# Turned rows for two FFN runs, smaller rings of drives and decays, and the gate's values in the hidden buffer, in a hybrid attention, FFN and state-space kernel

## The reference, cut to what matters

```python
x = x + attention(layernorm(x), ...)     # gated delta rule, 32 heads
x = x + ffn(layernorm(x), ...)           # layer 0 of the FFN
x = x + state_space(layernorm(x), ...)   # 16 states for each of 512 channels
x = x + ffn(layernorm(x), ...)           # layer 1, the same weights

def ffn(x):                              # weights unpacked from 4 bits, INNER = 1408
    gate, up = x @ w_gate.T, x @ w_up.T
    y = (silu(gate) * up) @ w_down.T
    return y / sqrt(mean(y * y, -1) + 1e-6)

def state_space(x):
    dt = softplus(x @ dt_w + dt_b); B, C = split(x @ bc_w.T + bc_b)
    h = exp(dt * A) * h + (dt * x) * B   # step by step along the sequence
    return (h * C).sum(states) @ out_w.T + out_b
```

## Time and profile before

| what | us |
|---|---|
| median of three runs | 4284.56 |
| the profiled execution | 4285.06 |
| its span | 4283.4 |
| joint stage with scans (3249 to 4113): length, PE busy, DVE busy | 864.0, 831.2, 786.5 |
| after the last scan (4113 to the end): length, PE busy, DVE busy | 170.4, 159.2, 23.1 |

### The profile page before, as it was taken

How to read it: one execution, slowest core, us unless ns; L and a number is a source line. 1 busy time by engine, 2 the same in 40 slices (tenths; PEclk the granted TensorE clock), 3 DMA queues, 4 the chain that set the end, 5 groups by cost and what they waited for, 6 DMA issues and landing times. The chain is left out here.

```text
span 4283.4 us, 82747 instructions
## 1 busy us (share of the span) xinstructions
PE 4131.2 (96%) x30773; PEld 2542.0 (59%) x30773; DVE 3402.7 (79%) x8648; ACT 2295.7 (54%) x5351; POOL 460.5 (11%) x470
## 2 busy tenths in 40 slices
PE   7899999999999999999999999998899999999999
PEld 4566666666666666666666666666444444444444
DVE  4888888888888888888888888886547989888950
ACT  3555555555555555555555555554445655554543
POOL 0111111111111111111111111111000000000000
PEclk9999999999999999999999999999999999999999
DMA  2111111111111012111011011010104445444520
GB/s 75 42 34 35 38 37 37 34 38 33 36 43 33 31 41 75 58 43 33 31 38 38 31 43 33 31 39 10 66 1 129 160 139 175 150 149 146 174 69 10
DMA packets 202467, 263.50 MB, mean 62 GB/s; under 512 B 18222, under 2 KB 101426, under 8 KB 202066
## 3 DMA queue, kind: packets, MB, share of 16 engines
q1 hardware_dynamic: 202066, 258.20, 18.9%
HBM read 249.24 MB, written 8.91 MB: 60 GB/s over the span
## 5 line engine op out<-in xcount | busy, mean ns | idle before, releaser
L516 PE MATMUL bank<-x_blocks,w_qkv 128*128 128x512 f32 x2048 | 927.3, 596 | 4.9 <-ACT raw L810 4.2
L516 PEld LDWEIGHTS bank<-x_blocks,w_qkv 128*128 128x128 f32 x2048 | 375.7, 192 | 394.5 <-issue 375.6
L1126 DVE SCALAR_TENSOR_TENSOR conv<-raw,conv_w,conv 128x1024 f32<-128x1024 f32 x384 | 516.1, 1344 | 71.2 <-ACT conv L784 62.1
L642 PE MATMUL bank<-w_out_unit,oT 128*128 128x512 f32 x1008 | 492.3, 611 | 15.2 <-ACT oT L858 15.2
L598 PE MATMUL bank<-w_z_unit,x_blocks 128*128 128x256 f32 x2048 | 488.5, 382 | 0.0
L598 PEld LDWEIGHTS bank<-w_z_unit,x_blocks 128*128 128x128 f32 x2048 | 372.0, 192 | 40.8 <-issue 0.2
L1371 PE MATMUL bank<-xnT_f,w_gu 128*128 128x512 f32 x704 | 330.3, 613 | 9.1 <-ACT xnT_f L1861 8.2
L810 ACT COPY raw<-bank 128x512 f32<-128x512 f32 x256 | 149.0, 582 | 323.7 <-PE bank L516 321.0
L1389 PE MATMUL bank<-w_down,hidden 128*128 128x512 f32 x704 | 319.5, 597 | 2.8 <-DVE hidden L1411 2.8
L1379 PE MATMUL bank<-xnT_f,w_gu 128*128 128x512 f32 x704 | 316.8, 593 | 0.6 <-DVE hidden L1411 0.5
L907 ACT ACTIVATE k_scaled<-o 128x128 f32<-128x128 f32 x512 | 153.9, 302 | 301.6 <-DVE o L1176 261.5
(11 more groups left out here) (245 smaller groups left out, 7785.1 us busy)
## 6 DMA issues: line engine op xcount, KB each, us to landing
rows_b<-bc_rows SPq DMA_DIRECT2D x256, 256.0 KB, 3.4
rows_c<-bc_rows SPq DMA_DIRECT2D x256, 256.0 KB, 3.5
w_qkv<-in_w_qkv SPq DMA_DIRECT2D x128, 256.0 KB, 2.9
decay<-gc_rows SPq DMA_DIRECT2D x64, 512.0 KB, 3.9
w_z_unit<-in_w_z SPq DMA_DIRECT2D x32, 512.0 KB, 4.4
w_out_unit<-in_w_out SPq DMA_DIRECT2D x32, 512.0 KB, 5.0
x_after<-x SPq DMA_DIRECT2D x16, 256.0 KB, 2.0
x_blocks<-x_after SPq DMA_DIRECT2D x4, 1024.0 KB, 10.1
```

Source lines behind the costliest of these rows:

```text
L516: made = e.matmul(PROJ[:, :], w_qkv[:, p % 2, j, :], xnT[:, n // HK, j, h * BANK:(h + 1) * BANK], start=j == 0, stop=j == KT - 1)
L642: made = e.matmul(out_rows(N, t)[:, :], turned_to(N, t)[:, r, :], w_out[:, N % 2, r, :], start=r == 0, stop=r == REP - 1)
L1126: e.scalar_tensor_tensor(acc, raw[:, i % 2, tap:tap + T], conv_w[:, tap, col:col + 1], acc, ALU.mult, ALU.add).then_inc(on["conv"], 1)
```

## The change

Seven things change, all in `second_half`:

1. `xnT_f` gets two buffers, by run parity, and `gate` is gone: silu writes into `hidden`, and the hidden product is made in place. silu no longer waits for the hidden product of the tile before, but for the down product of two tiles before. `drive` has 6 buffers in place of 8, `step_decay` 3 in place of 4.
2. The decay of step p + 2 therefore waits for the scan of step p - 1, in place of p - 2, and a drive for the sum of the pair six steps back, in place of eight.
3. `SUM_LAG` is 3 in place of 4: sums of pairs and the turns and copies of `y` come one slot earlier.
4. The four turns of a run stand in four slots (start - 5 to start - 2), all through WB, in place of two slots with two each (start - 4 and start - 3) through WB and the gate's bank.
5. Statistics come one slot earlier relative to the run's start, one tile per slot for runs 2 to 6.
6. `RUN_START` moves: run 2 from 43 to 46, run 3 from 91 to 92, run 4 stays at 136, run 5 from 183 to 184, run 6 from 230 to 235, run 7 from 279 to 281. The scans keep their slots (8 to 263).
7. In run 0's part the rows of run 1 are normalized and turned a little earlier, and run 0's last down product comes last.

```diff
-RUN_START = {1: 0, 2: 43, 3: 91, 4: 136, 5: 183, 6: 230, 7: 279}
-SUM_LAG, DRIVE_RING, H_RING = 4, 8, 3
+RUN_START = {1: 0, 2: 46, 3: 92, 4: 136, 5: 184, 6: 235, 7: 281}
+SUM_LAG, DRIVE_RING, H_RING, DECAY_RING = 3, 6, 3, 3
-        uses += [(at - 4 + t // 2, 1, ("ffn_turn", R, t)) for t in range(TILES)]
+        uses += [(at - 5 + t, 1, ("ffn_turn", R, t)) for t in range(TILES)]
-        xnT, xn = sb("xnT_f", [P, KT, BANK]), sb("xn_f", [P, 2, D])
+        xnT, xn = sb("xnT_f", [P, 2, KT, BANK]), sb("xn_f", [P, 2, D])
-        gate, hidden = sb("gate", [P, BANK]), sb("hidden", [P, 2, BANK])
+        hidden = sb("hidden", [P, 2, BANK])
...
 (silu_gate)
-            if U > 0:
-                e.wait_ge(on["hidden"], U)
-            e.activation(gate[:, :], GB[:, :], ACT.Silu).then_inc(on["gate_silu"], 1)
+            if U >= 2:
+                e.wait_ge(on["down_pe"], U - 1)
+            e.activation(hidden[:, U % 2, :], GB[:, :], ACT.Silu).then_inc(on["gate_silu"], 1)
 (make_hidden)
-            if U >= 2:
-                e.wait_ge(on["down_pe"], U - 1)
-            e.tensor_tensor(hidden[:, U % 2, :], UB[:, :], gate[:, :], ALU.mult).then_inc(on["hidden"], 1)
+            row = hidden[:, U % 2, :]
+            e.tensor_tensor(row, UB[:, :], row, ALU.mult).then_inc(on["hidden"], 1)
...
 (run 0's part, PE)
-                for t in range(TILES):
+                for t in range(2, TILES):
                     prepare(("turn1", t))
-                    if t == 0:
-                        down_mm(e, 0, IT - 1)
+                down_mm(e, 0, IT - 1)
...
-        stats_slot = {at - 8: R for R, at in RUN_START.items()}
+        stats_slot = {at - 9: R for R, at in RUN_START.items()}
-                    if i == 1:
-                        e.wait_ge(on["gate_silu"], IT * q)
-                    made = turn(e, turn_bank(i), xn[:, i % 2, :])
+                    made = turn(e, WB, xn[:, i % 2, :])
...
 (ACT, eviction of a turn)
-                    e.copy(xnT[:, :, i * P:(i + 1) * P], split(turn_bank(i))).then_inc(on["work_read"], 1)
+                    e.wait_ge(on["up_pe"], IT * (q - 1))
+                    e.copy(xnT[:, q % 2, :, i * P:(i + 1) * P], split(WB)).then_inc(on["work_read"], 1)
 (ACT, decay)
-                    if p + 2 >= 4:
-                        e.wait_ge(on["scan"], p - 1)
-                    e.activation(step_decay[:, (p + 2) % 4, :], dt[:, (KT * q + i) % 2, :], ACT.Exp,
+                    if p + 2 >= DECAY_RING:
+                        e.wait_ge(on["scan"], p + 3 - DECAY_RING)
+                    e.activation(step_decay[:, (p + 2) % DECAY_RING, :], dt[:, (KT * q + i) % 2, :], ACT.Exp,
...
 (DVE, statistics of runs 2 to 6, tile by tile)
+                for t in range(TILES):
+                    R = stats_slot.get(slot + TILES - 1 - t, 0)
+                    if 1 < R < len(RUNS) - 1:
+                        tile_stats(e, R, t)
+                if slot in stats_slot and stats_slot[slot] < len(RUNS) - 1:
+                    all_moments(e, stats_slot[slot])
+                elif slot in stats_slot:
                     ffn_stats(e, stats_slot[slot])
```

More of the change, by code:

```diff
@@ L1370, in gate_mm @@
             for j in range(KT):
-                made = e.matmul(GB[:, :], w_gu[:, j, i * P:(i + 1) * P], xnT[:, j, :], start=j == 0, stop=j == KT - 1)
+                made = e.matmul(GB[:, :], w_gu[:, j, i * P:(i + 1) * P], xnT[:, R % 2, j, :], start=j == 0,
+                                stop=j == KT - 1)
             made.then_inc(on["gate_pe"], 1)
@@ L1378, in up_mm @@
             for j in range(KT):
-                made = e.matmul(UB[:, :], w_gu[:, j, INNER + i * P:INNER + (i + 1) * P], xnT[:, j, :],
+                made = e.matmul(UB[:, :], w_gu[:, j, INNER + i * P:INNER + (i + 1) * P], xnT[:, R % 2, j, :],
                                 start=j == 0, stop=j == KT - 1)
@@ L1597, in tensor @@
                     e.wait_ge(on["prep_read"], prep_at[("piece", 2 * i + 1)] + 1)
+                    for t in range(2):
+                        if i == IT - 1:
+                            prepare(("turn1", t))
                     up_mm(e, 0, i)
@@ L1626, in evict @@
                     else:
[L1627 removed]
+                        place = {"turn0": xnT[:, 0, :, :], "turn1": xnT[:, 1, :, :], "dt_w": dt_wT, "out_w": out_wT}[kind]
                         made = e.copy(place[:, :, i * P:(i + 1) * P], split(bank))
@@ L1701, in vector @@
                         e.tensor_scalar(rate[:, :, :], rate[:, :, :], -1.0, None, ALU.mult).then_inc(on["ss_rate"], 1)
-                    if i == IT - 3:
+                    if i == IT - 4:
                         ffn_stats(e, 1)
-                for t in range(TILES):
-                    e.wait_ge(on["prep_made"], prep_at[("turn0", t + 2) if t < 2 else ("turn1", t - 2)] + 1)
-                    ffn_normed(e, 1, t)
+                    for t in range(TILES):
+                        if i == (IT - 3 if t < 2 else IT - 2):
+                            e.wait_ge(on["prep_made"], prep_at[("turn0", t + 2) if t < 2 else ("turn1", t - 2)] + 1)
+                            ffn_normed(e, 1, t)
             with nc.Block() as block:
@@ L1795, in work @@
                 last_out = kind == "out" and q == BLOCKS - 1
-                if last_out and i > 0 or kind == "ffn_turn" and i > 0:
+                if last_out and i > 0:
                     e.wait_ge(on["work_read"], k - 1)
@@ L2069, in vector @@
                     add_residual(e, residual_slot[slot])
-                if slot in stats_slot:
+                for t in range(TILES):
+                    R = stats_slot.get(slot + TILES - 1 - t, 0)
+                    if 1 < R < len(RUNS) - 1:
+                        tile_stats(e, R, t)
+                if slot in stats_slot and stats_slot[slot] < len(RUNS) - 1:
+                    all_moments(e, stats_slot[slot])
+                elif slot in stats_slot:
                     ffn_stats(e, stats_slot[slot])
```

19 lines of the change are left out of this document (10 added, 9 removed).

## The result

Over five runs each, the changed kernel takes 4299.77 us (4298.73 to 4301.49), the kernel before 4282.26 (4279.05 to 4285.48). The ratio is 1.0038, with a 95% interval of 1.0027 to 1.0050: slower by 17.5 us. The prediction called the change no change, by its own bound of 0.2%; the measured interval lies wholly above that. The time is inside the stated range, which is 44 us wide, but outside the 4282 to 4294 of the likeliest case: it is the case with a chance of 0.28, and nearest to the third rival's 4298.

A forecast was written before the change was run, and what follows sets the result against it. PE and DVE were taken as both at their limit among the scans, PE alone behind them. 12.1 - 1.3 - 4.5 - 1.0 - x, with x = -0.6, gave 5.9 us more: 4290.5 us, range 4260 to 4304.

The forecast's parts named there:

- likeliest case: Whole kernel: the forecast's own sum alone, without the rivals, holds 4282 to 4294 us; chance 0.36.
- third rival: Copies behind squares at runs 2, 3 and 5 and smaller rings hold DVE: x -8 to -9, 4298 us; chance 0.26.
- first rival: PE alone is the bound, only its pauses count and 25.0 us of them go: 4260 us; chance 0.30.
- Two engines at their limit, so slots are time: Joint stage with the scans: PE and DVE both full, so run 6's gate five slots later is 12 us later.
- Rings at 0: Smaller drive and decay rings among the scans: cost 0, since `carry` and `h` bind first; from above some 10 us.
- Run 0's part 1.0: End of run 0's part: a pause goes under the last down product, gain between 0 and 1.5, taken at 1.0 us.
- From run 6's first gate to run 7's: -5.8: Three sums fewer behind run 6's gate (-1.3 us), and run 7's start loses 6.9 in place of 11.4 (-4.5).
- First gate of run 6: 12.1 later: Run 6's start, slot 230 to 235: its gate starts at about 4020.5, 12.1 us later, less DVE's gain.
- x: DVE's gain in waiting up to slot 232: 8.0 less 8.6, so -0.6 us, between -14 and +20.
- the failed step: run 2's start: Slot 46: loss of 1.7 us from a gate ahead of the dt product, gain of 1.2 from a shorter `carry` wait.
- The other terms of x: Gains: run 6 3.0, run 5 2.0, run 3's statistics 1.8 us; losses: run 3 2.0 and 2.9, run 5 2.0.
- The signs: Trace checks: run 6's gate time, PE's idle ahead of it, DVE full behind it, run 7's wait of about 4 us, DVE's waits.

The follow-up runs named there:

- e3: The changed kernel with only run 2's start back at slot 43 in place of 46: 4283.72 us, ratio 1.0007.
- e2: The changed kernel with run starts put back near those of before (43, 92, 136, 183, 230, 280): 4279.80 us, ratio 0.9995.
- e1: The kernel before with only the smaller rings (drive 6, decay 3) and SUM_LAG 3: 4279.74 us, ratio 0.9994.
- m1: The changed kernel with only run 2's statistics, rows and turns three slots earlier, its gate staying at 46: 4290.29 us, ratio 1.0021.
- e5: The changed kernel with only run 6's squares and residual one slot later, behind the fourth copy of run 7's rows: 4295.20 us, ratio 1.0033.
- m2: The changed kernel with only run 1's squares and residual three slots later, behind all four copies of run 2's rows: 4296.55 us, ratio 1.0034.
- e6: The changed kernel with run 2's start at 47 in place of 46, the dt product of slot 46 ahead of the gate: 4300.40 us, ratio 1.0043.
- e10: The changed kernel with starts 43, 92, 136, 183, 230, 281 and run 6's squares and residual behind run 7's copies: 4271.24 us, ratio 0.9976.

## Why the prediction was right, and where it was wrong

The span is 15.4 us longer, the forecast was 5.9, and the 9.5 between them are nearly all one step.

- *PE's and DVE's work is the same.* Right: 4131.2 and 4135.6 us on PE, 3402.7 and 3403.1 on DVE.
- *Two engines at their limit, so slots are time.* Right. From run 6's start to the last scan (4029 to 4115) DVE is busy for 85.97 and PE for 84.91 of 86.00 us. The first rival, 4260 for PE alone as the bound, falls with it. e3 shows 16 us from three slots of one run, at equal work on both engines. The Trainium skill, in "Perfetto Trace Analysis", section "Identifying Performance Opportunities", says to optimize the engine with the highest occupancy first. It warns there that matmul busy time is no good measure of how close TensorE is to its limit, so the 96% alone did not make the first rival its forecast, as the prediction has it.
- *Silu into `hidden`, statistics tile by tile, two buffers: nothing.* Right, together (e2).
- *Rings at 0.* Right (e1). The upper bound of 10 was far too high.
- *Run 0's part 1.0.* It was 1.9 at the scan of slot 8, at the size of that place's spread (e3's and m1's execution reached it 4.5 us later than the changed kernel's, with the same code ahead of it), so not settled.
- *From run 6's first gate to run 7's: -5.8.* Measured -4.9 (148.1 against 153.0 us). At run 7 PE's loss was forecast at 6.9 in place of 11.4, by one wait for the copy behind the squares; counted the same way it is 11.4 - 4.3 = 7.1. e5 confirms the cause: with the squares behind the copy 4.6 of it go.
- *First gate of run 6: 12.1 later, less x and run 0's gain, so 11.7.* Measured 20.6 later. The scans tell x by itself: from slot 8 to slot 230 they lose 10.3 us (1.9 earlier to 8.4 later), so x was -10.3 where I had -0.6, and 12.1 + 10.3 - 1.9 gives the 20.5. The 12.1 is right, x was the fault.
- *x, the failed step: run 2's start.* I booked there a loss of 1.7, a gate ahead of the dt product, and a gain of 1.2, a shorter wait for `carry`: together 0.5. The scans of slots 42 to 48 lost 10.2. m1 and m2 split the 9.3 of it that m1 gave back: 3.6 are copies behind squares, 5.7 the turns behind the last down product. The dt product behind the gate is 1.1 (m1 against e3) to 1.8 (e6) at that place, so the 1.7 booked for it was right in size. What I had not done is ask what ACT does while it waits for the first turn: its order holds the decays and `carry` behind the copy, so a late turn isn't PE's loss alone, it stops the scans. For runs 3 and 5 I did weigh the squares; for run 2 the sum had dt only, and the squares stood in the third rival alone.
- *The other terms of x*, from slot 48 to slot 230: forecast to lose 0.1 in sum, measured 1.1. But these steps go up and down by 3 to 6 us between (10.2 later at slot 80, 14.4 at 128, 10.2 at 184, 14.7 at 192, 8.4 at 230), so the sum is right and its parts are not confirmed.
- *The signs.* Run 6's first gate 10 to 14 us later: missed, 20.6. PE standing still for 10 us or more ahead of it: just missed, 8.8. DVE full from there to the last scan, and one wait of about 4 us behind the squares before run 7's gate: both came (3.13 us). DVE's waits at 70 to 80 us, above 85 for the third rival: 83.8, between the two. No scan waited for a decay.
- *The third rival, 4298.* Its size is near what happened, x -8 to -9 against -10.3, and its time too. (Its own terms, 8.0 less 17.2, give -9.2 and 4299.) Its mechanism is right in its squares (3.6 at run 2, 4.6 at run 7, which the forecast had), wrong in its rings, and lacks the larger part, the turns behind the last down product. So its time came near in part by luck.

Open is why run 2's gate at 43 rather than at 46, with the same turns, gives 7 us more behind slot 60. m1's stretch 3500 to 3550 has a residual wait of 2.6 and an output wait of 2.2, e3's 0.8 and 1.7; that is 2.3 of it.

## What to carry to other kernels

When several engines follow fixed orders, ask of each step that becomes late which instructions stand behind its *consumer* on the consumer's engine. A copy that waits costs little on an engine that is half idle, unless the copy that another engine's next step needs stands behind it. In this kernel, at runs 2 and 5, the turns of the next run wanted to lie between the large products of the run before, ahead of its last one, and their copies ahead of that product's squares; e10, which moved one turn of four at run 6 and left two copies behind squares, gave nothing. And where two engines are full at once, a start that moves three slots later is not free even if no work is added: each start is a number to be measured.

## What the runs showed of the hardware

The low clock added most of its own length again to two long pauses of PE, and a short pause had no such price. Granted clock in the changed kernel around run 1's last down product (from 3351, after a pause of 3.87 us) and at run 7's gate (from 4177, after 3.13), columns as in the earlier trace rows:

```profile
3351.00:3357.00 6.00, 5.75 (x7) 2.49 (x8) 5.43 (x8) 0.00 (x0) 0.00 (x0) 0.52 0.58 180
...
4177.00:4183.00 6.00, 5.88 (x7) 2.52 (x8) 2.35 (x4) 1.35 (x2) 0.00 (x0) 0.52 0.46 172
```

and in m1 for the same down product, after a pause of 1.33 in place of 3.87:

```profile
3355.00:3359.00 4.00, 3.80 (x11) 1.83 (x12) 4.00 (x6) 0.19 (x2) 0.00 (x0) 1.00 0.57 181
```

The first two run at the lower level, 1.2 GHz, the third at 2.4. The down product that came behind 2.5 us more of standing still also ran 2.7 us longer (6.41 against 3.70). From start to start the two slow groups take 6.24 and 6.32 us in place of 3.43, 2.8 and 2.9 more. The price is not a fixed share of the pause: in m1 the 4.73 us ahead of the sum at 3364.51 were followed by a granted clock of 0.56 (3364.5 to 3368), and the sum, the turn and the gate behind it took 1.7 us more than at full clock.
